# A graph-attention kernel: normalising sums head by head on the scalar engine, and building the row pattern there from squared differences

## The reference

```
hn     = relu(layernorm(x))
h[a]   = hn @ W[a]                               # per head a
score  = leaky_relu(h[a]@a1[a] (row) + h[a]@a2[a] (column), 0.2), only where adj > 0
att    = softmax(score) over the columns
out    = elu(concat over heads of att @ h[a])
result = x + out
```

## Time and profile before

| | us |
|---|---|
| median of 3 runs (942.68 to 944.92) | 944.34 |
| the profiled execution: its own time | 940.65 |
| the profiled execution: its span | 938.7 |
| DVE busy in the span | 781.5 (83%) |
| PE busy | 625.6 (67%) |
| ACT busy | 467.2 (50%) |
| POOL busy | 451.0 (48%) |

### The profile page before, as it was taken

How to read it: one execution, slowest core, us unless ns; L and a number is a source line. 1 busy time by engine, 2 the same in 40 slices (tenths; PEclk the granted TensorE clock), 3 DMA queues, 4 the chain that set the end, 5 groups by cost and what they waited for, 6 DMA issues and landing times. The chain is left out here.

```text
span 938.7 us, 9287 instructions
## 1 busy us (share of the span) xinstructions
PE 625.6 (67%) x2178; PEld 363.9 (39%) x2178; DVE 781.5 (83%) x1767; ACT 467.2 (50%) x707; POOL 451.0 (48%) x1004
## 2 busy tenths in 40 slices
PE   0115766665766766657753695598957896978894
PEld 0003433433433434434432453355534453545442
DVE  3799999999989989989987675377958697989995
ACT  0217888888888888888881110012312231223322
POOL 3404444444444344344442666745767476746730
PEclk9967798899889889897895797789969798989897
DMA  8635999999999999999941666756868588868862
GB/s 290 236 134 194 395 402 414 413 414 418 415 413 419 414 411 413 415 415 408 407 157 47 192 183 170 228 155 199 241 208 266 167 262 258 261 211 255 278 218 91
DMA packets 86011, 269.53 MB, mean 287 GB/s; under 512 B 16129, under 2 KB 24321, under 8 KB 81218
## 3 DMA queue, kind: packets, MB, share of 16 engines
q1 hardware_dynamic: 66194, 203.13, 55.8%
q0 software_dynamic: 19760, 65.78, 24.0%
HBM read 243.49 MB, written 25.37 MB: 286 GB/s over the span
## 5 line engine op out<-in xcount | busy, mean ns | idle before, releaser
L327 DVE FIND_INDEX8 places<-ones,sb_adj_rows 128x8 uint32<-128x392 int32 (+6 forms) x240 | 337.3, 1413 | 0.0
L430 ACT ACTIVATE positive<-sb_adj_rows 128x3088 bf16<-128x3088 int32 (+3 forms) x96 | 266.2, 2773 | 0.0
L491 PE MATMUL psH<-sb_W,normedT 128*128 128x512 f32 x384 | 246.3, 734 | 1.7 <-ACT normedT L451 1.7
L1060 PE MATMUL psO<-weighted_h,ident 128*128 128x512 f32 x276 | 171.5, 710 | 25.1 <-issue 25.1
L832 POOL DMA_INDIRECT nodes<-table,column x138 | 140.8, 1020 | 66.1 <-issue 40.4
L483 PE MATMUL psT<-ident,normed 128*128 128x128 f32 x192 | 37.8, 329 | 199.7 <-ACT normed L444 199.7
L837 POOL DMA_INDIRECT nodes<-table,list_column x109 | 111.0, 1018 | 76.3 <-DVE list_column L945 45.0
L986 DVE TENSOR_TENSOR weighted_h<-nodes,psW 128x2048 f32<-128x2048 f32 (+5 forms) x74 | 139.5, 1925 | 0.0
L533 POOL TENSOR_TENSOR node_sum<-node_sum,h_rows 128x512 f32<-128x512 f32 x48 | 61.1, 1274 | 153.0 <-ACT h_rows L460 153.0
L1066 PE MATMUL psO<-weighted_h,to_row 128*128 128x512 f32 x218 | 127.0, 668 | 6.6 <-issue 4.4
L492 PEld LDWEIGHTS psS<-sb_Wa,normedT 128*128 128x128 f32 x384 | 84.6, 220 | 114.9 <-issue 114.9
(11 more groups left out here) (155 smaller groups left out, 852.7 us busy)
## 6 DMA issues: line engine op xcount, KB each, us to landing
sb_adj_rows<-in_adj_dram SPq DMA_DIRECT2D x36, 1344.0 KB, 13.4
sb_adj_rows<-in_adj_dram SPq DMA_DIRECT2D x36, 960.0 KB, 9.3
sb_adj_rows<-in_adj_dram SPq DMA_DIRECT2D x36, 576.0 KB, 6.6
table<-h_rows SPq DMA_DIRECT2D x48, 260.0 KB, 9.6
sb_x_rows<-in_x_dram SPq DMA_DIRECT2D x48, 256.0 KB, 9.8
x_part<-in_x_dram SPq DMA_DIRECT2D x19, 512.0 KB
out_dram<-result SPq DMA_DIRECT2D x19, 512.0 KB
sb_adj_rows<-in_adj_dram SPq DMA_DIRECT2D x10, 720.0 KB, 9.9
```

The lines of the kernel that those rows point to most:

```text
L327: ins = nc.vector.max_index(places[:, t % 2, 8 * s:8 * s + 8], sb["ones"][:, 0:8], adj_rows[:, u, a:b + SENTINELS])
L430: ins = nc.scalar.activation(positive[:, cols], adj_rows[:, u, cols], ACT.Relu, accum_out=sb["sums"][:, t, half:half + 1])
L491: nc.tensor.matmul(psH[:, t % 2], normedT[:, t % 2, kc], sb["W"][:, kc], start=(kc == 0), stop=(kc == KC - 1))
L1060: nc.tensor.matmul(psO[:, o, i], sb["ident"][:], weighted_h[:, u % 2, q], start=a, stop=False)
```

## The change

Two pieces of work move from DVE to ACT, and the order on DVE changes with them.

- `turn(u)` leaves DVE. On ACT each listed block gets one `Square` of (1 to 128) plus a bias that is minus the row number, into a new buffer `apart`, and then one `Relu` of 1 - square over all listed blocks of the unit makes `to_row`. For this `row_no` holds the negative number. It stands between `square(u+4)` and `facts_out(u+3)`.
- The product of `psO` and the reciprocals leaves DVE. In `grow(g)` ACT runs one `Identity` activation for every head of every tile (8 or 16 of them, 128 x 64 each, from PSUM), whose scale is that head's column of `recip`; then `below` and `grown` follow as before.
- DVE's `normalise` keeps only the reciprocal; `kept` goes into `finish`, ahead of `result`. At the end the last `normalise` comes ahead of the last two `finish`.

```diff
-            nc.gpsimd.iota(row_no[:], [[0, 1]], base=1, channel_multiplier=1, allow_small_or_imprecise_dtypes=True).then_inc(made, 1)
+            nc.gpsimd.iota(row_no[:], [[0, 1]], base=-1, channel_multiplier=-1, allow_small_or_imprecise_dtypes=True).then_inc(made, 1)
...
+            def turn(u):
+                if u >= U:
+                    return
+                w = UNITS[u]
+                if u >= 1:
+                    act.wait_ge(turned, u)
+                for q in range(w.rests):
+                    nc.scalar.activation(apart[:, q], edge_no[:, 1:P + 1], ACT.Square,
+                                         bias=looked(facts[:, u % AHEAD], w)[:, q, w.slots + 1:w.slots + 2]).then_inc(squared_rows, 1)
+                if u >= TURNS:
+                    act.wait_ge(summed, u - TURNS + 1)
+                act.wait_ge(squared_rows, sum(x.rests for x in UNITS[:u + 1]))
+                nc.scalar.activation(to_row[:, u % TURNS, 0:w.rests], apart[:, 0:w.rests], ACT.Relu, bias=1.0, scale=-1.0).then_inc(turned, 1)
+
             def grow(g):
-                w = GROUPED[g]
+                w, o = GROUPED[g], g % 2
+                act.wait_ge(recips, g + 1)
+                if g >= 2:
+                    act.wait_ge(kept_done, g - 1)
+                for i in range(w.n):
+                    for h in range(H):
+                        ins = nc.scalar.activation(agg[:, o, i, h * F:(h + 1) * F], psO[:, o, i, h * F:(h + 1) * F], ACT.Identity,
+                                                   scale=recip[:, o, i * H + h:i * H + h + 1])
+                ins.then_inc(agg_done, 1)
                 act.wait_ge(agg_done, g + 1)
...
@@ ACT's loop
                 square(u + 4)
+                turn(u + 2)
                 facts_out(u + 3)
...
@@ DVE
             def normalise(g):
                 w, u = group_of(g)
-                o = g % 2
                 dve.wait_ge(summed, u + 1)
-                nc.vector.reciprocal(recip[:, 0:w.n * H], psD[:, o, 0:w.n * H]).then_inc(recips, 1)
-                dve.wait_ge(recips, g + 1)
                 if g >= 2:
-                    dve.wait_ge(grown_done, g - 1)
-                nc.vector.tensor_tensor(by_head(agg, o, 0, w.n), by_head(psO, o, 0, w.n),
-                                        recip[:, 0:w.n * H].rearrange("p (a h) -> p a h", h=H).unsqueeze(3).to_broadcast([P, w.n, H, F]),
-                                        ALU.mult).then_inc(agg_done, 1)
+                    dve.wait_ge(agg_done, g - 1)
+                nc.vector.reciprocal(recip[:, g % 2, 0:w.n * H], psD[:, g % 2, 0:w.n * H]).then_inc(recips, 1)
+
+            def finish(g):
+                w, o = GROUPED[g], g % 2
                 dve.wait_ge(agg_done, g + 1)
                 dve.wait_ge(x_loaded[o], 16 * (g // 2 + 1))
                 nc.vector.scalar_tensor_tensor(kept[:, o, 0:w.n], agg[:, o, 0:w.n], 0.0, x_part[:, o, 0:w.n],
                                                ALU.max, ALU.add).then_inc(kept_done, 1)
-
-            def finish(g):
-                w, o = GROUPED[g], g % 2
                 dve.wait_ge(grown_done, g + 1)
...
                 weigh(u)
-                turn(u + 2)
                 if u >= 1 and UNITS[u - 1].last:
                     normalise(UNITS[u - 1].group)
+            normalise(UNITS[U - 1].group)
             finish(UNITS[U - 2].group)
-            normalise(UNITS[U - 1].group)
             finish(UNITS[U - 1].group)
```

More of the change, by code:

```diff
@@ L778, in attend_edges @@
         weighted_h = buf("weighted_h", [P, 2, BLOCKS, HF])
-        to_row = buf("to_row", [P, TURNS, RESTS, P])
+        to_row, apart = buf("to_row", [P, TURNS, RESTS, P]), buf("apart", [P, RESTS, P])
         score, weight = buf("score", [P, 3, BLOCKS, H]), buf("weight", [P, 2, BLOCKS, H])
-        recip, agg, below = buf("recip", [P, 2 * H]), buf("agg", [P, 2, 2, HF]), buf("below", [P, 2, HF])
+        recip, agg, below = buf("recip", [P, 2, 2 * H]), buf("agg", [P, 2, 2, HF]), buf("below", [P, 2, HF])
         x_part, grown, kept, result = (buf(n, [P, 2, 2, HF]) for n in ("x_part", "grown", "kept", "result"))
@@ L790, in attend_edges @@
         turned, weights, weighted, summed = sem("turned"), sem("weights"), sem("weighted"), sem("rows_summed")
-        weights_kept = sem("weights_kept")
+        weights_kept, squared_rows = sem("weights_kept"), sem("squared_rows")
         below_done, agg_done, grown_done, finished = sem("below_done"), sem("agg_done"), sem("grown_done"), sem("finished")
@@ L878, in facts_out @@
                 nc.scalar.activation(looked(facts[:, u % AHEAD], w), looked(psC, w), ACT.Copy).then_inc(facts_done, 1)
-            def grow(g):
-                w = GROUPED[g]
+            def turn(u):
[11 more added lines that the diff above has]
+                nc.scalar.activation(to_row[:, u % TURNS, 0:w.rests], apart[:, 0:w.rests], ACT.Relu, bias=1.0, scale=-1.0).then_inc(turned, 1)
+            def grow(g):
+                w, o = GROUPED[g], g % 2
[7 more added lines that the diff above has]
+                ins.then_inc(agg_done, 1)
                 act.wait_ge(agg_done, g + 1)
-                nc.scalar.activation(below[:, 0:w.n], agg[:, g % 2, 0:w.n], ACT.Relu, scale=-1.0).then_inc(below_done, 1)
+                nc.scalar.activation(below[:, 0:w.n], agg[:, o, 0:w.n], ACT.Relu, scale=-1.0).then_inc(below_done, 1)
                 act.wait_ge(below_done, g + 1)
-                nc.scalar.activation(grown[:, g % 2, 0:w.n], below[:, 0:w.n], ACT.Exp, scale=-1.0).then_inc(grown_done, 1)
+                if g >= 2:
+                    act.wait_ge(finished, g - 1)
+                nc.scalar.activation(grown[:, o, 0:w.n], below[:, 0:w.n], ACT.Exp, scale=-1.0).then_inc(grown_done, 1)
             act.wait_ge(made, 1)
@@ L892, in _ @@
             square(3)
+            turn(0)
+            turn(1)
             facts_out(2)
@@ L945, in front @@
                 nc.vector.tensor_scalar(column[:, u % AHEAD, 0:q], key[:, 0:q], -1.0, float(N + 1), ALU.mult, ALU.add).then_inc(columns, 1)
[L947 to L958, removed]
             def score_edges(u):
@@ L1016, in _ @@
             front(0)
-            turn(0)
             own(2)
             front(1)
-            turn(1)
             for u in range(U):
```

## The result

| us | before | changed |
|---|---|---|
| median of 4 runs each | 943.51 (942.37 to 944.92) | 959.23 (955.59 to 964.45) |
| profiled execution, its own time | 940.65 | 959.3 |
| span | 938.7 | 957.7 |
| DVE busy | 781.5 | 734.9 |
| ACT busy | 467.2 | 595.9 |

What follows compares the result with a forecast made beforehand. DVE was taken to bound the last part, PE just behind; afterwards a chain through ACT's products decides. Two-tile groups +17.2, tail +2.7, first half -2 gave +17.9 us on 944.3: 962 us, range 948 to 982.

Steps and rivals of the forecast that it cites:

- The chain: Second phase, reciprocal to reciprocal across ACT and DVE: six-block period from 9.56 to 10.9 us, eight blocks 12.0.
- The product: ACT's small products in grow: 0.24 us a start, sixteen 3.9 us (1.8 to 5.3), against 1.26 on DVE.
- The two-tile sum: Intervals between the 18 two-tile reciprocals, 734.11 to 920.47 us, each set to the larger of itself and the chain: +17.2 us.
- The tail: After the last sum, reciprocal to below goes from 1.55 to 4.2 us: +2.7 us.
- The first half: One-tile groups of the second phase: chain of 8.0 us against 8.55 between reciprocals; -2 us (bounds -8 and +3).
- rival (c): TensorE falls to 1.2 GHz behind longer PE gaps: +12 to +20 us on top, 974 to 982 us; chance 0.20.
- The pattern: Squares and Relu on ACT, 1.1 us for two blocks, hidden; removing 0.33 us from DVE helps only where DVE bounds.
- Rival (a): Small products on ACT are cheap, from 0.15 us each downward, and DVE decides: about -10 us, 934 us; chance 0.11.
- Rival (b): No change: PE's slow stretches hide both loss and gain, 944 us; chance 0.06.

Runs made afterwards that it cites:

- x3: Changed kernel with the products' scale a constant 0.5 in place of the per-partition reciprocal; ratio to the kernel before 0.9954 (0.9938 to 0.9969).
- x4: Changed kernel with every product also made a second time, ahead of it, into a bf16 buffer nobody reads; ratio to the kernel before 1.0841 (1.0808 to 1.0874).
- x6: Changed kernel with only DVE's finish of unit u-2 moved behind weigh of u; ratio to the kernel before 1.0350 (1.0279 to 1.0421).
- x5: Changed kernel reordered: DVE scores u+1 before the reciprocal, finish behind it; ACT's exponentials precede grow; ratios to the kernel before 1.0104 and 1.0014 in two sets.
- x1: Kernel before with only the pattern moved to ACT, the product with the reciprocals staying on DVE; ratio to the kernel before 0.9991 (0.9971 to 1.0011).
- x7: Changed kernel with one product of 512 per tile instead of eight of 64, head 0's reciprocal for all heads; ratio to the kernel before 1.0033 (1.0007 to 1.0059).

## Why the prediction was right

The direction and the mechanism were right, and the size came out close: 962 forecast, 959.2 measured. That it is so close is partly luck, since misses cancel. By its steps:

- **The chain** from reciprocal through ACT's products, below, grown, result and weigh: confirmed by the rows, by x3 and x4 (period follows the products by -1.41 and +3.27) and by x6 and x5 (order alone moves it by +1.4 and -2.3). Forecast 10.9 and 12.0 us, measured 10.34 and 11.41; DVE's idle time ahead of kept and result was forecast at about 3 us a unit, and 2.3 was measured.
- **The product** was the mis-sized term: 0.24 us a start was taken from squares, 0.20 was measured; sixteen take 3.38, not 3.9. The 0.55 us too much is the whole error of the period. The upper bound for one product alone (0.33) was passed by its duration, 0.356, while the starts overlap more.
- **The two-tile sum:** +17.2 forecast, +12.5 measured. In the last eight intervals, +13.6 forecast and +9.1 measured, it is that term (0.55 in each). In the nine before, +3.7 and +3.4 agree by luck: with the product at its true price the same sum gives +1.3, and longer waits for PE (9.85 us in one) make up the rest.
- **The tail:** +2.7 forecast, +2.4 measured, again the product.
- **The first half:** -2 forecast, +1.3 measured, and the second phase even began 1.9 us sooner than before. In the three pairs of traces its first two-tile reciprocal moved by +1.3, +0.6 and +3.6 us, inside the bounds of -8 and +3 twice and just outside once. Single intervals do shorten (663.85 to 672.26 before, 8.41 us; the same one is 7.35 in the changed kernel, where the chain's 8.0 allowed -0.5), but the next one, with a long wait at its end, grows from 17.36 to 24.41 us (waits 7.07 and 13.43). The waits for PE took the gain.
- **Left out of the sum:** +2.8 us before the last reciprocal. PE had stood idle and began the last unit at the half clock (pairs of 2.04 us, then 0.96). The same piece is 7.39 and 5.72 us in the two later traces of the changed kernel, so it varies from run to run. This is what rival (c) describes, once, where nothing hides it. Its mechanism was at work before that too: PE runs at the half clock in every second six-block unit (912 to 919 us below), and yet over the eight intervals before (851.53 to 934.28) the reciprocals stand 10.34 or 10.35 apart. One cold spell fits into the slack, as the prediction said, and up to there no spell cost more. In the mean the granted clock fell from 0.90 to 0.86.

```profile
912.00:919.00 7.00, 6.36 (x13) 3.39 (x14) 3.68 (x9) 5.06 (x18) 0.42 (x1) 0.53 0.46 158
```

- Two misses cancel: the product too dear by some 5 us, and the first half and the last unit too cheap by 6. And the forecast added 3.7 us because the median of the kernel before was that much above its profiled run; the changed kernel's median is 0.1 below its own, so the +17.9 stands against +18.7 in the profiled runs and +15.7 in the medians.
- **The pattern** was taken as hidden on ACT and worth 0.33 on DVE where DVE decides: period -0.35 in x1; but x1 is no faster as a kernel (0.9991).
- **Rival (a)** fell by the operand: x3 shows 0.11 us a start with a constant scale, below the 0.15 from which it would decide, and 0.20 was measured with the reciprocal. **Rival (b)** fell in three sets: the lower ends of the ratios are 1.0143, 1.0083 and 1.0099.
- ACT's busy time rose by 129 us (about 140 forecast), DVE's fell by 47 (about 50).

Between x3's constant scale and the changed kernel's per-partition one lie 0.09 us a start ((3.38 - 1.97) / 16). The Trainium skill ("ScalarE: Activation LUTs", What ACT_TABLE_LOAD costs) states about 93 ns for each such operand in the time of one instruction. The trace agrees in the pace, 88 ns a start; in the mean duration it has 64 ns (356 against 292).

## What to carry to other kernels

Before moving work from a full engine to an idle one, write down the loop from one instruction to its next instance across all engines and put the moved work into it: an engine that is 30% busy can still be the one that everybody waits for. A wide instruction with a broadcast operand that is split into many with a per-partition scale pays mostly for its starts: here sixteen took 3.38 us, and in x7 two over the same elements 1.26. And if the work can be taken out of the loop by reordering, look at what is next: here it was TensorE's slow stretches, and they kept all of the gain in the two sets where that was run.

## What the runs showed of the hardware that was not expected

- ACT, products 128x64 out of PSUM: 0.356 us each and 0.20 from start to start with a per-partition scale; 0.292 and 0.11 with a constant. Durations overlap by some 0.16 to 0.18 us, more than the 0.09 of the squares that read SBUF. A duration alone says little of the pace.
- The same program took 878 us in one set and 939 to 946 in three others. The granted TensorE clock from 580 to 734 us was 0.92 to 0.95 there and 0.80 to 0.85 here, and the waits without a named releaser (89 to 145 us ahead of ACT's facts_out) were absent there.
- PE can be slower than at its half clock while the clock shown is nearly full: 1.62 of 6 us busy, its gaps marked `issue`, at a granted clock of 0.97 (721 to 727 us of the kernel before).
